# Self attention with keys as rows: scores taken twice, the maximum as two more contraction rows, no transposed probabilities

## The reference

```python
h = _layernorm(x, ln1_g, ln1_b)
q = (h @ sa_wq.T + sa_bq)   # k and v likewise; split in 16 heads of 32
scores = jnp.einsum('bhqd,bhkd->bhqk', q, k) * HD ** (-0.5)
p = jax.nn.softmax(scores, axis=-1)
o = jnp.einsum('bhqk,bhkd->bhqd', p, v)
x = x + (o @ sa_wo.T + sa_bo)
```

## Time and profile before

| what | us |
|---|---|
| median of 3 runs | 3689.26 |
| profiled execution, own time | 3688.11 |
| its span | 3686.3 |
| PE busy | 3448.7 (94%) |
| DVE, ACT busy | 1816.3, 1802.7 (49% each) |
| POOL busy | 1138.8 (31%) |
| `L1sa`: first transfer to last store issued | 1261.4 to 2434.1 |

### The profile page before, as it was taken

One profiled execution on the slowest core, in us unless ns is written; L12 is line 12 of the kernel. 1 busy time (PEld: TensorE's weight loads), 2 busy tenths in 40 slices (PEclk: granted clock), 3 DMA queues, 4 the chain that ended last, 5 costly groups with the idle time before them and its releaser, 6 DMA issues. The chain is left out here.

```text
span 3686.3 us, 51567 instructions
## 1 busy us (share of the span) xinstructions
PE 3448.7 (94%) x18384; PEld 2905.3 (79%) x18384; DVE 1816.3 (49%) x3472; ACT 1802.7 (49%) x4868; POOL 1138.8 (31%) x1576
## 2 busy tenths in 40 slices
PE   4899979999999799999999999977999989999999
PEld 3788858888888578888888888855888768888887
DVE  3566644222222277777777767745666442222221
ACT  2677634222222266666667667735667542222222
POOL 2455521111111134444434435414455311111110
PEclk8999989999999899999999999988999989999999
DMA  3112123111111232322322332321221131111010
GB/s 95 39 58 71 61 83 99 39 35 35 35 35 35 72 92 72 101 74 75 94 80 69 94 91 59 92 69 53 76 72 48 52 112 52 35 35 35 35 35 35
DMA packets 158341, 232.91 MB, mean 63 GB/s; under 512 B 35894, under 2 KB 53510, under 8 KB 158086
## 3 DMA queue, kind: packets, MB, share of 16 engines
q1 hardware_dynamic: 158086, 229.63, 20.7%
HBM read 115.45 MB, written 41.94 MB: 43 GB/s over the span
## 5 line engine op out<-in xcount | busy, mean ns | idle before, releaser
L1060 POOL TENSOR_SCALAR L1sa_Pr<-L1sa_Pr,L1sa_rinv 128x512 f32<-128x512 f32 x512 | 354.8, 702 | 595.7 <-DVE L1sa_rinv L942 595.7
L102 DVE TENSOR_TENSOR L1sa_PTl<-L1sa_t,L1sa_PTh 128x512 fp32r<-128x512 f32 x512 | 352.2, 688 | 193.2 <-ACT L1sa_PTh L96 183.5
L96 ACT ACTIVATE L1sa_PTh<-L1sa_t 128x512 fp32r<-128x512 f32 x512 | 305.6, 597 | 266.2 <-PE L1sa_o L91 251.2
L846 ACT ACTIVATE L1sa_Pr<-L1sa_s,L1sa_nmax 128x512 f32<-128x512 f32 x512 | 350.9, 685 | 77.8 <-DVE L1sa_nmax L934 72.3
L934 DVE TENSOR_REDUCE L1sa_nmax<-L1sa_s 128x1 f32<-128x512 f32 x512 | 346.9, 678 | 17.7 <-PE L1sa_s L709 17.7
L89 PE MATMUL L1sa_o<-L1sa_PTh,L1sa_Vbh 128*128 128x256 f32 x1024 | 330.4, 323 | 3.5 <-DVE L1sa_oTl L103 2.1
L422 DVE TENSOR_TENSOR L0ff_gl<-L0ff_gf,L0ff_gh 128x512 fp32r<-128x512 f32 x128 | 95.2, 743 | 475.3 <-ACT L0ff_gh L382 475.3
L422 DVE TENSOR_TENSOR L1ff_gl<-L1ff_gf,L1ff_gh 128x512 fp32r<-128x512 f32 x128 | 95.8, 749 | 473.1 <-ACT L1ff_gh L382 473.1
L723 PE MATMUL L1sa_t<-ident,L1sa_Pr 128*128 128x128 f32 x2048 | 312.2, 275 | 14.0 <-DVE L1sa_PTl L102 12.8
L723 PEld LDWEIGHTS L1sa_t<-ident,L1sa_Pr 128*128 128x128 f32 x2048 | 243.5, 141 | 92.8 <-DVE L1sa_PTl L102 24.5
L368 ACT ACTIVATE L0ff_gf<-L0ff_f,cols 128x512 f32<-128x512 f32 x128 | 88.3, 690 | 451.0 <-PE L0ff_f L91 451.0
(11 more groups left out here) (296 smaller groups left out, 9380.3 us busy)
## 6 DMA issues: line engine op xcount, KB each, us to landing
L1sa_stack_q<-L1sa_parts_q SPq DMA_DIRECT2D x256, 128.0 KB, 2.7
L1sa_stack_k<-L1sa_parts_k SPq DMA_DIRECT2D x256, 128.0 KB, 2.7
L0ff_xs<-x SPq DMA_DIRECT2D x64, 256.0 KB, 3.5
L1sa_xs<-x SPq DMA_DIRECT2D x64, 256.0 KB, 3.5
L1ff_xs<-x SPq DMA_DIRECT2D x64, 256.0 KB, 3.5
L0ca_xs<-in_x SPq DMA_DIRECT2D x32, 256.0 KB, 3.6
L0ca_stage<-in_x SPq DMA_DIRECT2D x32, 256.0 KB, 3.9
x<-L0ca_stage SPq DMA_DIRECT2D x32, 256.0 KB, 2.0
```

The costliest lines, as they stand in the source:

```text
L96: return nc.scalar.activation(hi, bank, ACT.Copy)
L102: return nc.vector.tensor_tensor(lo, bank, f32(hi), ALU.subtract)
L846: nc.scalar.activation(Pr[:, h % 2, qt, :], s_bank[s % S_BANKS][:, :], ACT.Exp, bias=nmax[:, h % 2, qt:qt + 1], accum_out=rsum[:, h % 2, q ...
L1060: nc.gpsimd.tensor_scalar(p, p, rinv[:, h % 2, qt:qt + 1], 0.0, ALU.mult, ALU.add)\
```

## The change

Only `self_attention` changes (and `Count` gets a method `no`). All other stages are the same instructions.

- The scores are computed twice. `scores` as before, for the maximum alone. `scores_T` computes them a second time with keys as rows and queries as columns; in this form the maximum of each query would be a number for each column, which ACT's bias cannot be. So the negated maximum, split in high and low (`m_split`, POOL), is transposed by PE (`m_transposed`), copied from PSUM by ACT (`m_copy`), and carried by a transfer of SP (`m_rows`) into two more rows of `stack_q`, with ones in `stack_k`: the matmul of 98 rows subtracts it.
- `exp` works on 128 keys x 2 x 512 queries at once and its result `E` is already what the second product wants. It is split into `Eh` and `El` on ACT, DVE and POOL, by the tables `EH_BY` and `EL_BY`. The transposes, `p_hi`, `p_lo` and `normal` are gone.
- V of one head is the stationary operand of 96 columns: high, low and ones, in turn (`Vst`, `place_v`). One matmul gives V high, V low and the sum of the exponentials, 96 rows; there are two passes, with `Eh` and with `El`, so 4 matmuls of 512 columns for 2 x 128 keys. ACT copies the 96 rows out (`o_out`), a transfer (`line_up`) puts high, low and sum of 32 rows beside each other, and once in four heads POOL adds and scales (`o_sum`, `o_scaled`) and DVE inverts the sum (`o_inverse`, 128 x 512).
- A batch now has 32 steps n, half a head each. In step n PE does `scores_T(n+2)`, `scores(n+6)`, projection pieces, `PV(n)` with `Eh`, in even steps `m_transposed` of head n/2+2, pieces, `PV(n)` with `El`. `SA_ORDER` names the order of the projection units, and `sa_pieces` spreads their quarters (three matmuls) evenly over the 64 half steps; the four layer norm transposes count as a quarter each.
- `scores` and `scores_T` have two banks each, both written in one step and both read by one instruction.
- SP's transfers: for each head and each of q and k one of 64 rows and one of 32 rows; before there were two of 64 rows. `m_rows` and `line_up` are added, one each a head. Their order is written out with the steps.

```diff
+SA_ORDER = ([("q", 0, 2), ("k", 0, 2)] + [("O", -1, t) for t in range(TT)] + [("q", 0, 3), ("k", 0, 3)]
+            + [("T", 1, c) for c in range(KT)] + [("q", 1, 0), ("k", 1, 0)] + [("V", 1, t) for t in range(TT)]
+            + [("q", 1, 1), ("k", 1, 1)])
+SA_FIRST = [("T", c) for c in range(KT)] + [("q", 0), ("k", 0)] + [("V", t) for t in range(TT)] + [("q", 1), ("k", 1)]
+STEPS = H * 2
+
+
+def sa_pieces():
+
+    quarters = [(*u, c) for u in SA_ORDER for c in range(1 if u[0] == "T" else KT)]
+    halves = [[] for _ in range(2 * STEPS)]
+    for i, q in enumerate(quarters):
+        halves[i * 2 * STEPS // len(quarters)].append(q)
+    return halves
...
-        stack = {n: ph.sb(f"stack_{n}", [P, 2, 4, S], F32R) for n in "qk"}
+        KD, KM = 3 * HD, 3 * HD + 2
+        stack = {n: ph.sb(f"stack_{n}", [P, 8, S], F32R) for n in "qk"}
         parts = {n: ph.sb(f"parts_{n}", [P, 2, S], F32R) for n in "qk"}
-        Vh, Vl = (ph.sb(n, [P, TT, D], F32R) for n in ("Vh", "Vl"))
-        Vbh, Vbl = (ph.sb(n, [P, TT, 4, P], F32R) for n in ("Vbh", "Vbl"))
-        Pr = ph.sb("Pr", [P, 2, TT, S])
-        PTh, PTl = (ph.sb(n, [P, 2, S], F32R) for n in ("PTh", "PTl"))
-        nmax, rsum, rinv = (ph.sb(n, [P, 2, TT]) for n in ("nmax", "rsum", "rinv"))
+        V = ph.sb("V", [P, TT, 2, D], F32R)
+        VS = 5
+        Vst = ph.sb("Vst", [P, TT, VS, HD, 3], F32R)
+        E = ph.sb("E", [P, 2, 2 * S])
+        Eh, El = ph.sb("Eh", [P, 2, 2 * S], F32R), ph.sb("El", [P, 2, 2 * S], F32R)
+        nmax = ph.sb("nmax", [P, 2, TT])
+        mm = ph.sb("mm", [P, 2, 2 * TT], F32R)
+        mT = ph.sb("mT", [2 * TT, 2, P], F32R)
+        osb = ph.sb("osb", [3 * HD, S])
+        OLN = ph.sb("OLN", [P, 3, S])
...
+        onorm = x.htmp
...
+        LEAD_S, LEAD_T = 6, 2
...
+        EH_BY, EL_BY = ("act", "act", "act", "pool"), ("pool", "dve", "pool", "dve")
...
-        QK_STEPS = {(0, 1, 0): (0, 1, 2, 2), (0, 1, 1): (2, 2, 3, 4), (0, 2, 0): (15, 15, 16, 17),
-                    (0, 2, 1): (18, 18, 18, 18), (0, 3, 0): (24, 25, 26, 27), (0, 3, 1): (34, 34, 34, 34),
-                    (1, 0, 0): (45, 46, 47, 47), (1, 0, 1): (48, 48, 49, 49)}
-        O_STEPS = ((5, 6, 6, 7), (7, 8, 8, 9), (10, 10, 11, 12), (12, 13, 13, 14))
-        T_STEPS = (35, 37, 39, 41)
-        V_STEPS = ((50, 50, 50, 50), (51, 52, 53, 54), (55, 56, 56, 57), (58, 59, 59, 60))
...
+            def m_rows(h):
+                sp.wait_ge(e_mc.sem, e_mc.no(h))
+                sp.dma_start(f32(stack["q"][KD:KM, h % 8, :].rearrange("a (t n) -> a t n", t=TT)),
+                             f32(mT[:, h % 2, :])).then_inc(e_m[h % 2].sem, 16)
+
+            def line_up(h):
+                sp.wait_ge(e_ob.sem, e_ob.no(h))
+                if h % 4 == 0 and h > 0:
+                    sp.wait_ge(e_on.sem, e_on.no(h // 4 - 1))
+                sp.dma_start(OLN[HD * (h % 4):HD * (h % 4 + 1), :, :],
+                             osb[:, :]).then_inc(e_oln.sem, e_oln.unit)
...
+                for n in steps_of(b):
+                    s = n % STEPS if n >= 0 else n
+                    if n % 2 and 0 <= (n + 3) // 2 < HEADS:
+                        m_rows((n + 3) // 2)
+                    if n % 2 == 0 and n >= 2:
+                        line_up((n - 2) // 2)
+                    if n < 0:
+                        continue
+                    for step, kind, ahead, g, pair in ((3, "q", 0, 2, 0), (5, "k", 0, 2, 0), (6, "q", 0, 2, 1),
+                                                       (6, "k", 0, 2, 1), (14, "q", 0, 3, 0), (14, "q", 0, 3, 1),
+                                                       (16, "k", 0, 3, 0), (16, "k", 0, 3, 1), (20, "q", 1, 0, 0),
+                                                       (22, "k", 1, 0, 0), (22, "q", 1, 0, 1), (22, "k", 1, 0, 1),
+                                                       (31, "q", 1, 1, 0), (31, "q", 1, 1, 1), (0, "k", 0, 1, 0),
+                                                       (0, "k", 0, 1, 1)):
...
+            def scores(n):
+                h, slot = n // 2, n // 2 % 8
+                if n % 4 == 0:
+                    pe.wait_ge(e_stack[n // 4 % 4].sem, e_stack[n // 4 % 4].no(n // 16))
+                if n > 0:
+                    pe.wait_ge(e_mx.sem, e_mx.no(n - 1))
+                for i in range(2):
+                    qt = 2 * (n % 2) + i
+                    last = nc.tensor.matmul(s_bank[:, i, :], stack["q"][0:KD, slot, qt * P:(qt + 1) * P],
+                                            stack["k"][0:KD, slot, :], start=True, stop=True)
+                last.then_inc(e_s.sem, e_s.unit)
+
+            def scores_T(n):
+                h, slot = n // 2, n // 2 % 8
+                if n % 2 == 0:
+                    pe.wait_ge(e_m[h % 2].sem, e_m[h % 2].no(h // 2))
+                if n % 2 and (n + 1) // 2 < HEADS:
+                    pe.wait_ge(e_mc.sem, e_mc.no((n + 1) // 2))
+                elif n > 0:
+                    pe.wait_ge(e_ex.sem, e_ex.no(n - 1))
+                for i in range(2):
+                    kt = 2 * (n % 2) + i
+                    last = nc.tensor.matmul(st_bank[:, i, :], stack["k"][0:KM, slot, kt * P:(kt + 1) * P],
+                                            stack["q"][0:KM, slot, :], start=True, stop=True)
+                last.then_inc(e_st.sem, e_st.unit)
+
+            def m_transposed(h):
+                pe.wait_ge(e_mm.sem, e_mm.at(h, 1))
+                if h > 0:
+                    pe.wait_ge(e_ex.sem, e_ex.no(2 * h - 2))
+                nc.tensor.transpose(st_bank[0:2 * TT, 0, 0:P], f32(mm[:, h % 2, :]), cst.ident[:, :])\
+                    .then_inc(e_mt.sem, e_mt.unit)
+
+            def PV(n, low):
+                h = n // 2
+                if low:
+                    by = EL_BY[n % 4]
+                    pe.wait_ge(e_el[by].sem, e_el[by].no(kth(EL_BY, n)))
...
+                    if 0 <= n + LEAD_T < PAIRS:
+                        scores_T(n + LEAD_T)
+                    if n + LEAD_S < PAIRS:
+                        scores(n + LEAD_S)
+                    for half in range(2):
+                        if n >= 0:
+                            for kind, ahead, i, c in halves[2 * (n % STEPS) + half]:
+                                if exists(b + ahead):
+                                    piece(kind, b + ahead, i, c)
+                            PV(n, half == 1)
+                        if half == 0 and n % 2 == 0 and 0 <= n + 4 < PAIRS:
+                            m_transposed((n + 4) // 2)
...
+                act.wait_ge(e_st.sem, e_st.no(n))
+                if n < 2:
+                    act.wait_ge(wt.lo.sem, wt.lo.at(CHUNKS - 1, 0))
+                else:
+                    by = EL_BY[(n - 2) % 4]
+                    act.wait_ge(e_el[by].sem, e_el[by].no(kth(EL_BY, n - 2)))
+                nc.scalar.activation(E[:, n % 2, :], flat(st_bank[:, :, :]), ACT.Exp).then_inc(e_ex.sem, e_ex.unit)
+
+            def o_out(h):
+                act.wait_ge(e_pv.sem, e_pv.no(2 * h + 1))
+                if h > 0:
+                    act.wait_ge(e_oln.sem, e_oln.no(h - 1))
+                nc.scalar.activation(osb[:, :], o_bank[h % 2][0:KD, :], ACT.Copy).then_inc(e_ob.sem, e_ob.unit)
...
+                for n in steps_of(b):
+                    if n % 8 == 3 and n >= 11:
+                        o_hi((n - 11) // 8)
+                    if n % 2 == 0 and n >= 2:
+                        o_out((n - 2) // 2)
+                    if 0 <= n + 1 < PAIRS and EH_BY[(n + 1) % 4] == "act":
+                        e_hi(n + 1)
+                    if 0 <= n + LEAD_T < PAIRS:
+                        exp(n + LEAD_T)
+                    if n >= 0:
+                        for kind, b_of, i in evacs[n]:
+                            if kind != "O":
+                                evacuate(kind, b_of, i)
+                    if n % 2 == 0 and 0 <= n + 4 < PAIRS:
...
+            def e_lo(n):
+                by = EH_BY[n % 4]
+                dve.wait_ge(e_eh[by].sem, e_eh[by].no(kth(EH_BY, n)))
+                if n >= 2:
+                    dve.wait_ge(e_pv.sem, e_pv.no(n - 2))
+                nc.vector.tensor_tensor(El[:, n % 2, :], E[:, n % 2, :], f32(Eh[:, n % 2, :]), ALU.subtract)\
+                    .then_inc(e_el["dve"].sem, 1)
+
+            def o_inverse(g):
+                dve.wait_ge(e_oln.sem, e_oln.no(4 * g + 3))
+                nc.vector.reciprocal(OLN[:, 2, :], OLN[:, 2, :]).then_inc(e_ri.sem, e_ri.unit)
...
+                    if n + LEAD_S < PAIRS:
+                        maximum(n + LEAD_S)
+                    if n % 8 == 3 and n >= 11:
+                        o_lo((n - 11) // 8)
+                    if 0 <= n + 1 < PAIRS and EL_BY[(n + 1) % 4] == "dve":
+                        e_lo(n + 1)
...
+            def e_lo(n):
...
+                nc.gpsimd.tensor_tensor(El[:, n % 2, :], E[:, n % 2, :], f32(Eh[:, n % 2, :]), ALU.subtract)\
...
+            def m_split(h):
```

(20 more changed lines are left out.)

822 lines of the change are left out of this document (336 added, 486 removed).

## The result

The changed kernel took 3781.95 us (median of 4 runs, 3776.99 to 3796.18), the kernel before 3688.45 (4 runs, 3686.32 to 3692.94) on the same chip: ratio 1.0258, 95% interval 1.0228 to 1.0288. It is 2.6% slower; forecast were 3635 us, in a range of 3515 to 3735, and a faster kernel. The profiled execution took 3784.08, its span is 3782.3.

What follows compares the result with a forecast made beforehand. PE's own instructions were taken to bound self attention: 109.8 us a batch plus waits made 134.0 against 141.2. With start and tail, 54.5 us came off the profiled 3688.1: 3635 median, range 3515 to 3735.

Steps and rivals of the forecast that it cites:

- rival 3: Self attention loop: PE's clock could be 0.97, 25 us more, 3660; counted within the forecast's range, no chance of its own.
- PE's instructions, 109.8 us a batch: Self attention: matmuls at 0.23 us each plus small transposes sum to 109.8 us a batch, against 141.2 before.
- Waits, 24.2 a batch: PE's waits in the loop, added to 109.8 for 134.0 a batch: 7.2 - 1.8 + 8.0 + 10.0 + 0.8.
- For `m_rows` 10.0: PE waits for maximum rows behind stack copies in SP's queue: 4.3 (step 22), 2.1 (step 6), 3.6 (step 0).
- For the layer norm 8.0: Steps 15 and 16: next batch's transposes and q product wait 1.9, 2.2 and 3.9 us, in 7 batches.
- `m_transposed` was to wait 5.4: Even steps: it waits for `exp` of the same step, 0.9 x 8 = 7.2 a batch, less 1.8 replaced by `m_rows` waits.
- The output projection 0.8: Step 3: the first output quarter waits 0.8 us a batch for `o_lo` after POOL's scaling.
- Rival 1: PE's waits overlap: half of them gives 3547 us, none with the tail hidden 3447; chance 0.27 for 3447 to 3590.
- Rival 2: POOL and DVE exclude each other, POOL sets the pace: 147 a batch, 3742 us; chance 0.22 together with rival 4.
- Rival 4: Matmuls with 96 stationary columns or `m_transposed` cost 10 a batch more: about 3700 us; chance 0.22 together with rival 2.
- The 37 us of waits before the change: Kernel before, self attention stage: PE's waits for the low parts come to some 37 us, each at most 1.0.
- balance of 31.4 us saved: Self attention: if nothing but PE's instructions counted, a batch would fall by 31.4 us, from 141.2 to 109.8.

Runs made afterwards that it cites:

- e12: Changed kernel with useless 512-column matmuls in all seven long PE waits of a batch, 98 a batch: 3724.98 us, 1.0095 of the kernel before.
- e8: e7 with 38 useless 512-column matmuls a batch in the three long PE waits left: 3616.42 us, 0.9806 of the kernel before.
- e2: Changed kernel with 50 useless matmuls a batch ahead of the waiting `scores_T` in steps 2, 8, 20 and 24: 3745.48 us, 1.0152 of the kernel before.
- e1: Changed kernel with the maximum rows' transfer issued by ACT behind its copy instead of by SP: 3675.47 us, 0.9966 of the kernel before.
- e10: Changed kernel with only SP's queue reordered, bursts of stack copies cut into fours behind the maximum rows: 3687.92 us, 1.0003 of the kernel before.
- e4: Changed kernel with all low parts `El` made by DVE, none by POOL: 3825.81 us, 1.0378 of the kernel before.
- e7: e5 plus DVE's normalisation moved above its `El` in step 14 and separate semaphores for q and k stack copies: 3649.80 us, 0.9907 of before.
- e9: Changed kernel with DVE's inversion of the denominators replaced by a copy of the same size: 3765.82 us, 1.0227 of the kernel before.
- e5: e1 plus the four layer norm transposes spread over steps 15 to 17, q product from step 18: 3673.27 us, 0.9964 of the kernel before.

## Why the prediction was wrong

The forecast was wrong in time and in sign. The step that failed is the price of PE's clock: the sum took all matmuls at 0.23 us and so the clock at nothing, and rival 3 allowed it 25 us; it cost some 92. The waits were short by 43 us as well, and with their measured length but a full clock the change would have been about neutral (139.4 us a batch by the sum, 141.6 in e12, 141.2 before).

Of the 147 us between forecast and result some 9 lie ahead of the first PV (1339.8 instead of 1331), 8 x 16.9 = 135 in the loop, the rest behind.

- **PE's instructions, 109.8 us a batch: right.** 0.23 us between starts at 96 and 98 rows too; e8 shows the sum within 1% at the full clock. That it is so close is in part luck: `m_transposed` was taken at 0.3 us and costs PE 0.1 (at 1869.87 it and the next matmul take 0.34 until the one after, and 0.23 of them are the matmul's), 3 us a batch less. A busy time counts the modelled end of the last matmul ahead of each wait, which goes the other way.
- **PE's clock: the step that failed most.** Rival 3 took 0.97 for the loop, read off windows by their busy share, so 25 us in all. It was 0.90: 11.5 us a batch, 92 us over eight, most of it clock (in e8 and e12, at 1.00 and 0.99, PE's busy time is still 1.1 and 1.7 over what was counted). The idle time came in long pieces, mostly six a batch of 3.0 us and more, 24 us together, each with some us at half speed behind it. e2, e12 and e8 show that idling is the cause, by filling the pieces. That their length counts beside their share is only suggested: e1 and e10 idle 19.1 and 19.7 us a batch, with 3.0 and 3.7 pieces of 2.9 us and more, at 0.94 and 0.91. And shorter ones can be followed by the lower clock too (1.8 us in e4).
- **Waits, 24.2 a batch: 29.6.** For `m_rows` 10.0 were taken, 16.6 came. The mechanism was right (0.64 us an issue for copies of 32 rows as well, steps 24, 8 and 2), but the wait in step 20 was missed: there a `line_up` that is itself waiting and four loads stand ahead. For the layer norm 8.0 were taken, 9.6 came, of which 4.1 for DVE's normalisation, which stood behind an `El` and wasn't in the chain. `m_transposed` was to wait 5.4 and waited 1.0. It comes behind a late `scores_T`, but even without the waits for `m_rows` it waits only 2.2 (e7), where 7.2 were taken; the 5.1 of e1 hold another wait. The output projection 0.8, measured 2.0: `oTl` took 1.8 us instead of 0.75. DVE's inversion took 3.34 instead of 1, above the 2.7 given as its most, but isn't what the output projection waits for (e9).
- **Rival 1 (waits overlap)** was true of pairs of waits only: e5 and e7 show two, where the next in line took over.
- **Rival 2 (POOL and DVE exclude each other, POOL sets the pace)** came nearest in time (3742) for a wrong reason. Its own terms (111, 16, 8, 4 and 12) even add up to 151 and not to 147, which would be 3774; that this lies beside the result is luck. The exclusion is there. The changed kernel's timeline of DVE and POOL, and its groups of `oTl` (ns min/median/max) and POOL's `El`, in the window:

```profile
1644.76 2.38 POOL L1046 TENSOR_TENSOR L1sa_El<-L1sa_E,L1sa_Eh 128x1024 fp32r<-128x1024 f32 x1 [5.32 <-ACT L1sa_Eh L847]
...
1646.32 1.37 DVE L106 SCALAR_TENSOR_TENSOR L1sa_oTl<-L1sa_htmp,cols,L1sa_oTh 128x512 fp32r<-128x512 f32 x1
```

```profile
L106 DVE SCALAR_TENSOR_TENSOR L1sa_oTl<-L1sa_htmp,cols,L1sa_oTh x24: 1366/1832/2009, 1528.9 to 2398.0; 128x512 fp32r<-128x512 f32 x24
```

```profile
L1046 POOL TENSOR_TENSOR L1sa_El<-L1sa_E,L1sa_Eh x96: 2365/2397/3038, 1500.2 to 2396.7; 128x1024 fp32r<-128x1024 f32 x96
```

`oTl`, now with two operands in SBUF, ended 0.55 us after POOL's `El` had (0.5 to 0.6 in all eight looked at, from 1528 to 1798), and took 1.83 at the median where it took 0.75 with one in PSUM. The rule of the Trainium skill (SBUF — State Buffer, Who interferes with whom) is borne out here. But POOL is busy 56% of the window, its `El` is rarely held up (2.40 us at the median, 2.37 at least), PE waited for POOL's `El` 0.6 us in the whole stage, and in e4, with 24 us a batch taken off POOL (and put on DVE), nothing got faster.
- **Rival 4** is out: matmuls cost what was counted, and `m_transposed` less.
- The 37 us of waits before the change add PE's (12.8) and its weight loads' (24.5); PE itself was idle 28 us in that window. The forecast doesn't rest on it.
- The sum said faster because each wait was priced at its own length. With the clock, the waits cost 1.4 times their length (11.5 on 29.6; 1.5 times if all of it is put down to the 24 us of long ones), and the balance of 31.4 us saved against waits and clock of 41.1 comes out as it did: 9.7 us a batch slower.

## What to carry to other kernels

When a change takes work off a saturated PE, the freed time can come back as gaps, and here a gap of 3 us or more cost its length and a stretch at half clock behind it; price both, and look at where the idle time lies and how long each piece is, not only at its share. A small transfer on the critical path doesn't belong behind bulk copies in the same queue: reordering that one table gave back 94 us. Before mending a second wait, ask who is next in line within a step: in e5 and e7 the next took over nearly all of the gain.

## What the runs showed of the hardware

- Useless matmuls in a wait were worth their place here: 400 of them made the kernel 36 us faster, 266 in e8 33 to 37 us.
- DVE's reciprocal of 128 x 512 takes 3.34 us, its copy 0.73 at the median, its subtraction of twice the columns 1.22.
- Copies within SBUF cost SP 0.59 to 0.68 us to issue, for 4 KB as for 128 KB (now and then 1.1 to 1.7); ACT issues the 4 KB in 0.62.
